# Counting products of a graph kernel that stream two rows' columns instead of one

## The reference

```python
# layer 0: for each edge, then the maximum over a node's edges
h = x @ W1 + b1
m = relu(concat(h[dst], h[src] - h[dst]) @ W2 + b2)
m = relu(m @ W3 + b3)
x = layernorm(x + relu(segment_max(m, dst)))
# layer 1: attention over the edges and a loop at each node, twice
h = x @ W;  e = leaky(h@att_src [src] + h@att_dst [dst])
out = segment_sum(softmax_by_dst(e) * h[src], dst) + bias
x = layernorm(x + relu(...))
```

## Time and profile before

| | us |
|---|---|
| median of 3 runs | 5763.31 |
| lowest and highest run | 5754.06 to 5776.48 |
| span of the profiled execution | 5744.4 |
| TensorE busy in it | 4395.5 (77%) |
| VectorE busy | 4053.4 (71%) |
| ScalarE busy | 2772.7 (48%) |
| GpSimd busy | 2154.4 (38%) |

### The profile page before, as it was taken

How to read it: one execution, slowest core, us unless ns; L and a number is a source line. 1 busy time by engine, 2 the same in 40 slices (tenths; PEclk the granted TensorE clock), 3 DMA queues, 4 the chain that set the end, 5 groups by cost and what they waited for, 6 DMA issues and landing times.

```text
span 5744.4 us, 99002 instructions
## 1 busy us (share of the span) xinstructions
PE 4395.5 (77%) x35974; PEld 3827.1 (67%) x35974; DVE 4053.4 (71%) x6352; ACT 2772.7 (48%) x3925; POOL 2154.4 (38%) x2116
## 2 busy tenths in 40 slices
PE   4388878778778787887855848889887848888884
PEld 2266666666666666666644638888886637888884
DVE  4255555555555565555636949999996949999998
ACT  1033333333333333333322029999994009999996
POOL 4765556556566665665651030011111030001111
PEclk9677878788888888888877969999998979999997
DMA  4356555556566665665552622122221632112221
GB/s 133 110 167 171 165 160 165 166 159 170 161 172 171 178 176 169 170 172 172 171 151 97 230 66 61 57 60 66 62 64 52 230 114 52 57 57 69 60 63 50
DMA packets 764462, 717.37 MB, mean 125 GB/s; under 512 B 97095, under 2 KB 632703, under 8 KB 764152
## 3 DMA queue, kind: packets, MB, share of 16 engines
q1 hardware_dynamic: 424822, 319.77, 18.6%
q10 hardware_dynamic: 271394, 258.61, 16.0%
q0 software_dynamic: 67936, 135.03, 8.5%
HBM read 536.76 MB, written 176.36 MB: 124 GB/s over the span
## 4 chain that ended last, share of the span: by engine, by line
PE 29%; DVE 23%; issue 22%; another core or an unknown queue 14%; ACT 8%; ACTq 2%; POOL 1%; DMA 0%; SPq 0%; DVEq 0%; POOLq 0%
DVE ring_b L1250 13%; PE ps L1455 10%; DVE work L1239 5%; PE ps L1428 5%; PE ps L1418 5%; PE ps L1438 2%; PE ps L1417 2%; ACT ring_a L707 2%; PE ps L1583 2%; ACT work L786 1%; DVE work L1146 1%; ACT tab_flat L676 1%; ACT work L783 1%; POOL P_compact L578 1%
## 5 line engine op out<-in xcount | busy, mean ns | idle before, releaser
L557 POOL DMA_INDIRECT ring_a<-Q_table,late x1563 | 1648.1, 1054 | 1096.7 <-PE ps L1418 534.1
L1583 PE MATMUL ps<-tab_flat,ring_b 128*128 128x129 f32 x12152 | 1488.8, 280 | 77.4 <-DVE ring_b L1250 74.9
L1583 PEld LDWEIGHTS ps<-tab_flat,ring_b 128*128 128x128 f32 x12152 | 1424.8, 195 | 119.8 <-DVE ring_b L1250 117.7
L1035 DVE TENSOR_TENSOR_SCAN work<-ring_b,work,ps 128x512 f32<-128x512 bf16 x391 | 498.4, 1275 | 1042.6 <-remote 761.5
L1455 PEld LDWEIGHTS ps<-work,tab_flat 128*128 128x128 bf16 x7936 | 790.4, 143 | 605.9 <-issue 584.0
L1455 PE MATMUL ps<-work,tab_flat 128*128 128x49 bf16 x7936 | 900.2, 273 | 319.8 <-ACT ring_a L707 220.2
L1239 DVE TENSOR_TENSOR work<-work 128x1024 f32<-128x1024 f32 (+1 forms) x784 | 931.1, 1188 | 115.2 <-ACT work L786 111.7
L783 ACT ACTIVATE work<-work,scores 128x1024 f32<-128x1024 f32 (+1 forms) x784 | 879.5, 1122 | 133.8 <-DVE ring_b L1250 108.3
L1250 DVE SCALAR_TENSOR_TENSOR ring_b<-work,ring_a 128x1024 f32<-128x1024 f32 (+1 forms) x784 | 928.9, 1185 | 2.1 <-PE ps L1583 1.9
L786 ACT ACTIVATE work<-work,slope_src 128x1024 f32<-128x1024 f32 (+1 forms) x784 | 868.0, 1107 | 0.0
L707 ACT ACTIVATE ring_a<-ps 128x490 uint8<-128x490 f32 x806 | 469.3, 597 | 823.9 <-remote 432.0
(11 more groups left out here) (247 smaller groups left out, 4748.3 us busy)
## 6 DMA issues: line engine op xcount, KB each, us to landing
work<-P_compact SPq DMA_DIRECT2D x1563, 64.0 KB
work<-low_rows SPq DMA_DIRECT2D x312, 320.0 KB, 3.7
ring_b<-rank_rows ACTq DMA_DIRECT2D x194, 512.0 KB
run_max<-tab_flat ACTq DMA_DIRECT2D x194, 512.0 KB
ring_a<-counts SPq DMA_DIRECT2D x98, 896.0 KB, 5.0
counts<-ring_a ACTq DMA_DIRECT2D x62, 784.0 KB
ring_a<-Q_table,late POOLq DMA_INDIRECT x1563
ring_a<-counts SPq DMA_DIRECT2D x14, 672.0 KB, 4.3
```

What stands on the lines that cost most here:

```text
L557: pool.indirect_dma_start(out=q_ring[:, g % RING, j - j0, :], out_offset=None, in_=Q_table, in_offset=bass.IndirectOffsetOnAxis(ap=srcT_i[ ...
L1583: m = tensor.matmul(sums_of(tau), lhsT=a_ring[:, u % RINGA, (tau - a) * P:(tau - a + 1) * P], rhs=tab[:, h, 0:F + 1], start=(h == 0 and (t ...
```

## The change

Each counting product streams, beside its own row's 49 columns, the 49 columns of the next row, and writes 98 columns of the bank. The second half holds a meaningless product (one row's weights with the next row's columns), and the next product, which starts there, overwrites it. The last product of a batch streams 49 columns as before, so the bank ends with the same contents and nothing is written beyond it.

```diff
@@ fill_bank
                 r0, r1 = row_batches[b]
                 tensor.wait_ge(hot_made, batch(tau * RB + b + 1))
                 for k in range(r1 - r0):
-                    m = tensor.matmul(bank[:, k * NB:(k + 1) * NB], lhsT=hot_rows[:, hot_slot[b], :, k],
-                                      rhs=hot_cols[:, hot_slot[b], :, k], start=True, stop=True)
+                    e = min(k + 2, r1 - r0)
+                    m = tensor.matmul(bank[:, k * NB:e * NB].rearrange("p (r h) -> p r h", h=NB), lhsT=hot_rows[:, hot_slot[b], :, k],
+                                      rhs=hot_cols[:, hot_slot[b], :, k:e].rearrange("p h r -> p r h"), start=True, stop=True)
                 m.then_inc(bank_filled, 1)
```

## The result

The changed kernel took 5924.85 us in the median of 4 runs (5895.39 to 5952.55), beside 5769.9 us (5754.06 to 5796.67) for the kernel before: a ratio of 1.0276, 95% interval 1.0234 to 1.0317.

The account below looks back on a forecast made before the run. TensorE was taken to bound the counting stage most of the time, transfers second. Of 656 us more work, 78% (512 us) less a fifth gave +410; 5763 + 410 = 6173, rounded to 6170 us, range 5950 to 6480.

Parts of the forecast that it names:

- The pace of a product: Counting products on TensorE: 49 more columns cost 92 ns more each; ten products take 1.7 to 1.8 us at either clock.
- The three readings: Rows on counting products, read as showing that the moving operand's columns, 20 bytes apart, set the 92 ns.
- Where it shows: About +410 us in the counting stage and nothing elsewhere; stages after 2921 us shift and keep their length.
- How much reaches the end: Of 656 us more TensorE work, 78% on the chain, 512 us, less a fifth: about +410 us.
- The bound below: Least growth of the counting stage if every TensorE gap closes: 2052 + 656 - 2652 = 56 us.
- the one above: Most growth of the counting stage, if TensorE's gaps stay: 656 us.
- the section on the time before: Prediction's account of the counting stage: TensorE bounds it most of the time; 25.9% of the chain, 687 us, waits for landings.
- Rival 2: Counting stage: slack of POOL, DMA and ACT nearly covers the added work; +56 to +200 us, say 5890 us; chance 0.10.
- Rival 1: Counting products: 98 columns still go in 92 ns and the clock gains; 5696 us; chance 0.12.
- Rival 3: Counting stage: the clock falls too, low share of f32 work from 35% to 60%, 191 us; 6360 us; chance 0.16.
- The signs: Counting stage about 3060 us, L1455 above 30% of chain, DMA about 0.52, POOL waits over 700 us, clock 0.78 to 0.86.

Follow-up runs that it names:

- e12_more_instructions: Kernel before plus eight long-met waits after each batch on VectorE and on ScalarE; 5030.5 us beside 5025.7, and 5031.0 beside 5026.1.

## Why the prediction was wrong, by its steps

**The pace of a product** was right in each point: 98 columns at 182 ns, 1.7 us a batch, at either clock, the last product at 90. The three readings that gave it (the packed products, the clock that changes nothing, the load that starts with the product) are borne out by the packed layout's 58 ns. I used 656 us where 642 was measured.

**Where it shows**: one stage, the rest at 2823 and 2824 us. Right.

**How much reaches the end** is the step that failed: "78% of L1455 is on it, hence 512 us. From that I take off a fifth". The bound below, +56, and the one above, +656, hold the +155; the choice between them was wrong. Two mistakes are in it. First, a share of the chain before is no estimate for added work that lies beside idle time: the more TensorE has to do, the more of the delays around it pass while it works, and 335 of its 525 idle us went. Second, I took the chain's 687 us of "unknown queue" for landings of transfers that are issued ahead, as the section on the time before has it, and discounted a fifth. The waits that the view calls "remote" were waits for TensorE's own signals, raised up to 12 us behind the work. While TensorE has a batch of 1.7 us before it, part of that delay passes beside work and not beside idle time: the scans' lateness fell from 678 to 416 us. The unnamed share of the chain fell to 10.6%, in the direction that I had named, but by 387 us and not by 102.

**Rival 2**, that the gaps take most of it (+56 to +200 us, chance 0.10), was the outcome. What I held against it, that a longer product does not mend products that come one at a time, was wrong: 88 such pairs became one. **Rival 1** fell with the pace; a clock rise there was, 0.82 to 0.86 in the stage, but beside less idle time and not beside free columns. **Rival 3** had the wrong sign for this change. Of L1417's products the share at the low clock stayed (0.323 us in the mean, then 0.326), the W3 products' mean fell from 728 to 669 ns.

**The signs** I had named were mixed: L1456 at 41.6% of the chain, DMA share 0.56 (I had said about 0.52), POOL at 725 us, the clock just at the edge of 0.78 to 0.86. The stage's length alone, 2829 instead of 3060 us, was off.

That +410 is right on a chip Q (+404) is luck: there the bound is POOL, which the profile I read could not show. What stays open is why TensorE's signals and some of its products are late on a chip S. It is not the number of bytes that the kernel moves. Three rivals are untested: the number of transfers; the number of TensorE's own instructions; and the recording itself. For the last there is one sign, not a proof. Of the 392 times that VectorE raised the semaphore of the placing matrix, the trace of the kernel before has 149 on the chip S, and that of `e12_more_instructions` 381 on a chip Q. Every execution on record has its span and its clock, so each was recorded, and none shows a chip S without that.

## What to carry to other kernels

Before pricing added work by its share of the chain, subtract what its engine's idle time can take: the gaps are a pool that is used up once. A wait that a view calls "remote" should be held against the code's own waits, and against the moment at which each semaphore was raised, before it is called a transfer: here it was a signal of TensorE. And a moving operand read at a step of 20 bytes was priced by the column, 1.8 ns each, where 98 packed columns took 59 ns in all; but making it packed cost the VectorE operation that writes it six times its time.

## What was not expected of the hardware

Two kinds of chips run the same program in 5030 and in 5770 us. Most of the difference is in one stage (2093 against 2652 us); 64 us lie ahead of it and 98 behind it (2725 against 2823). On one kind TensorE's semaphores are raised up to 12 us behind the end that the profile gives its product, on the other 0.015 us, while VectorE's and ScalarE's are raised within 0.013 us on both. With nothing late, TensorE's clock in the stage is 0.96 instead of 0.82: the lateness seems to cost twice, once as a gap and once as a lower clock, which is argued and not tested. A bf16 operation of VectorE over 490 elements went from 404 to 2388 ns when only its output's step changed, and POOL's gathers beside it from 1050 to 1720 ns.
